# Attention: the two rows of a step added into one bank, half of each head's 16 output rows for each

## The chip, the cores and the metric

One NeuronCore of one Trainium2 chip runs the whole program in one launch. The metric is the device time in microseconds (us), the median of several executions. Its engines are TensorE (PE, with its weight loads as PEld), VectorE (DVE), ScalarE (ACT), GpSimd (POOL) and SyncE (SP), which here issues most of the transfers.

## What is computed

The program is a triangular-attention block followed by an MLP and a four-way Mamba block on x of shape (2, 64, 64, 256), float32. The change is in the attention:

```python
B, N, _, E = x_in.shape            # 2, 64, 64, 256
H = 8; d_k = E // H                # 32
q, k, v1, v2 = ((x_in @ W).reshape(B, N, N, H, d_k) for W in (Wq, Wk, Wv1, Wv2))
scores = jnp.einsum('bilhd,bljhd->biljh', q, k) / np.sqrt(d_k)
att = jax.nn.softmax(scores, axis=2)
out = jnp.einsum('biljh,bilhd,bljhd->bijhd', att, v1, v2)     # this line
attn_out = out.reshape(B, N, N, E) @ Wo
```

For each pair of heads, image b and row i, `out[i, j, d]` is a sum over l of `att[l, j] * v2[l, j, d] * v1[i, l, d]`: the elementwise product of the first two is formed for every d, and the sum over l, weighted with v1, is a matrix product.

## The kernel before

The attention works on one pair of heads at a time (4 pairs, `PAIRS`), and 128 partitions hold (head of the pair, l). For each pair there are two chunks c, one per image b, 8 in all (`NC`). A chunk has 64 rows i, taken two at a time: 32 steps a chunk, 256 steps t in all, one main loop on each engine.

In a step, DVE and POOL share the elementwise product (`product`, L306): DVE makes `av[t % 2][:, both rows, d 0..21, j]` from att and `v2ps` (in PSUM), POOL makes d 22 to 31 from `v2sb`. The two `av` buffers let them run one step ahead of PE: `need(dve, i_done, 2 * t - 2)` holds product t until the matmuls of step t - 2 are done. PE (`row`, L473 to L486) sums over l. The 32 values of d are cut into 4 strips of 8; for one row i, strip s is one fp32 matmul with 128x32 weights `w[:, i, s, :]` and 512 moving columns (8 d, 64 j), and its result goes to partitions 32 s to 32 s + 31 of a bank, so that the four strips of a row use four different quarters of the array's columns. The strips 0 and 1 need only DVE's part of `av`; strip 2 is the first that waits for POOL. Each fp32 matmul of this kind shows in the trace as two passes, each a weight load and a matmul.

The weights are v1 with one column per (head, d) and zeros for the other head: of the 32 columns of a strip, 8 are used for head 0 (0 to 7), 8 for head 1 (16 to 23); the others hold zeros. So a bank holds one row i, and half of its 128 partitions hold zeros; within a partition only the 64 columns of its own d are wanted. ACT copies each bank whole to `ev` (`evict`, L646 to L655), one copy a row. `ev` has two buffers of `EB` = 4 banks. When four rows are in a buffer, SP stores them (`store`, L258 to L265) with 8 DMAs of 8 partitions, 4 rows and 64 columns each. A store must have landed before its buffer is used again (`o_stored`).

There are 3 banks for the rows (`NB`). The weights are built by ACT from v1 (`build`), 8 rows at a time in two copies, one for each head.

In the same loop, for the next pair of heads, PE computes the scores (`scores`, L461: 16 groups of 8 matmuls of 64x64 tiles, in steps 0 to 10 of a pair, one and two groups in turn) and later the transposes of att (`turn`, L471, 16 groups of four); ACT copies the scores, takes the exponentials and copies the transposed att; DVE finds the minima and inverts the sums (L356, L365), POOL normalises (L327). This is so in the first three pairs (steps t 0 to 191); the last pair has only its own work. At the end of a chunk ACT copies the next chunk's v2 to `v2ps` in three pieces (`turn_v2`), each as soon as DVE has read the old one; DVE's first product of the new chunk is in three pieces too, each waiting for its copy.

SP's queue is in order: per chunk the loads of the chunk after (`load_v2`, two halves of `load_v1`) stand between the stores. Each engine runs its program in the order of the code; nothing else sets it. At the very end half of the last store is issued from ACT (`store_last`), and SP waits at L297 for every store to land; then the block ends on all engines and the MLP block begins.

## Time and profile before

| | |
|---|---|
| median of 3 runs | 2349.0 us (2346.99 to 2353.96) |
| the profiled execution | 2351.3 us, its span in the profile 2349.5 us |
| main loop of the attention, first to last matmul of L485 | 258.9 to 1092.7 us of the span |
| first matmul of the MLP block | 1099.8 us |
| DVE, PE, ACT, POOL busy over the span | 85%, 87%, 55%, 58% |

Times in the rows count from the start of the span. A busy PE in the table is a count of overlapping matmul records, not of work done. "x" is the number of instructions merged in a row. What ended an engine's idle time stands behind the arrow.

### The profile page before, as it was taken

What the parts mean: (1) busy time and instruction counts of PE and PEld (TensorE: products, weight loads), DVE (VectorE), ACT (ScalarE), POOL (GpSimd) and SP (SyncE); (2) the same over time, 40 slices, a digit from 0 to 9 for tenths busy, and PEclk for the clock granted to TensorE, in tenths of its full rate; (3) what the DMA queues carried; (4) which work ended last, traced back from release to release, by engine and by line L of the source; (5) the groups of instructions that cost most, each with busy time, mean ns of one, the idle gap of its engine ahead of it and who ended that gap; (6) DMA issues with size and microseconds to landing.
All of it is one profiled execution on the core that took longest, in us unless ns stands there. A gap on an engine that the chain in (4) does not pass through costs nothing. (4 is left out here: it accounts for less than half of the span.)

```text
span 2349.5 us, 43512 instructions
## 1 busy us (share of the span) xinstructions
PE 2033.5 (87%) x17008; PEld 1405.1 (60%) x17008; DVE 2001.5 (85%) x2292; ACT 1303.9 (55%) x2840; POOL 1358.6 (58%) x734
## 2 busy tenths in 40 slices
PE   8989977787788776665999997999999999999997
PEld 7868522232233221111787875888888888888886
DVE  4426799989999999996798885899989999999997
ACT  3337667767766785543232244656565665555553
POOL 1103699989998999996011001455555555666553
PEclk9999999999999999998999998999999999999997
DMA  6768512122321212301134222343222333433432
GB/s 233 249 216 237 145 33 55 42 56 46 66 54 29 38 20 38 94 17 27 54 101 137 81 64 59 68 88 81 74 73 73 90 82 97 108 91 93 105 93 64
DMA packets 300828, 203.98 MB, mean 87 GB/s; under 512 B 202064, under 2 KB 278864, under 8 KB 296528
## 3 DMA queue, kind: packets, MB, share of 16 engines
q1 hardware_dynamic: 282304, 146.51, 25.8%
q0 software_dynamic: 8704, 33.56, 3.9%
q10 hardware_dynamic: 9616, 21.14, 3.1%
q8 instruction: 135, 2.21, 0.4%
q14 instruction: 69, 0.57, 0.1%
HBM read 133.24 MB, written 67.90 MB: 86 GB/s over the span
## 5 line engine op out<-in xcount | busy, mean ns | idle before, releaser
L306 DVE TENSOR_TENSOR att_av<-att_att,att_v2ps 128x2816 f32<-128x2816 f32 (+2 forms) x288 | 775.6, 2753 | 29.4 <-PE att_bank L485 26.5
L306 POOL TENSOR_TENSOR att_av<-att_att,att_v2sb 128x1280 f32<-128x1280 f32 x256 | 744.3, 2933 | 45.6 <-PE att_bank L485 41.5
L485 PE MATMUL att_bank<-att_av,att_w 128*32 128x512 f32 x4096 | 551.0, 617 | 213.0 <-DVE att_av L306 189.8
L485 PEld LDWEIGHTS att_bank<-att_av,att_w 128*32 128x32 f32 x4096 | 138.6, 111 | 563.6 <-issue 282.7
L651 ACT ACTIVATE att_ev<-att_bank 128x512 f32<-128x512 f32 x512 | 296.8, 595 | 262.4 <-PE att_bank L485 218.3
L1864 DVE SCALAR_TENSOR_TENSOR mb_cv<-mb_bank,mb_cw,mb_cv 128x504 f32<-128x504 f32 (+2 forms) x480 | 351.5, 733 | 58.9 <-ACT mb_cv L1658 47.5
L1463 POOL TENSOR_TENSOR mb_y_lo<-mb_y,mb_y_hi 128x1024 fp32r<-128x1024 f32 x60 | 142.5, 2396 | 257.9 <-DVE mb_S L1873 257.9
L1534 PE MATMUL mb_bank<-dt_xT_hi,dt_win_hi 128*128 128x512 f32 x576 | 233.3, 405 | 27.5 <-DVE mb_cv L1864 24.4
L1534 PE MATMUL mb_bank<-dt_xT_lo,dt_win_hi 128*128 128x512 f32 x576 | 226.2, 393 | 0.0
L1534 PE MATMUL mb_bank<-dt_xT_hi,dt_win_lo 128*128 128x512 f32 x576 | 225.9, 392 | 0.0
L1658 ACT ACTIVATE mb_cv<-mb_bank,mb_cw 128x512 f32<-128x512 f32 x160 | 110.0, 690 | 194.6 <-PE mb_bank L1534 193.1
L1469 POOL TENSOR_TENSOR mb_S<-mb_S,mb_dskip 128x512 f32<-128x512 f32 x124 | 158.2, 1296 | 8.5 <-DVE mb_S L1880 8.5
L1873 DVE TENSOR_TENSOR_SCAN mb_S<-mb_dAb,mb_inj 128x512 f32<-128x512 f32 x128 | 149.7, 1211 | 3.2 <-DMA mb_dAb<-dA_rows 3.2
L1534 PEld LDWEIGHTS mb_bank<-dt_xT_hi,dt_win_hi 128*128 128x128 f32 x576 | 109.2, 190 | 62.1 <-DVE mb_cv L1864 38.5
L1446 POOL TENSOR_TENSOR mb_inj<-mb_diag,dt_dt 128x512 f32<-128x512 f32 x128 | 129.7, 1046 | 13.1 <-DVE mb_S L1873 13.0
L1676 ACT ACTIVATE mb_xc<-mb_cv,mb_cb 128x512 f32<-128x512 f32 x128 | 91.7, 716 | 69.3 <-DVE mb_cv L1864 69.3
L606 ACT ACTIVATE att_raw<-att_raw,att_least 128x64 f32<-128x64 f32 x384 | 128.5, 339 | 0.8
L1594 PE MATMUL mb_bank<-dt_wf_hi,mb_y_hi 128*128 128x256 f32 x512 | 128.8, 291 | 0.0
L1594 PE MATMUL mb_bank<-dt_wf_lo,mb_y_hi 128*128 128x256 f32 x512 | 126.0, 286 | 0.0
L1534 PEld LDWEIGHTS mb_bank<-dt_xT_hi,dt_win_lo 128*128 128x128 f32 x576 | 109.0, 189 | 24.1
L1004 PE MATMUL mlp_bank<-mlp_w,mlp_hid 128*128 128x256 f32 x512 | 118.4, 382 | 3.6 <-ACT mlp_hid L1081 3.6
L1534 PEld LDWEIGHTS mb_bank<-dt_xT_lo,dt_win_hi 128*128 128x128 f32 x576 | 109.2, 190 | 19.6
(199 smaller groups left out, 3864.4 us busy)
## 6 DMA issues: line engine op xcount, KB each, us to landing
att_xin<-in_x SPq DMA_DIRECT2D x32, 512.0 KB, 4.4
qk_t<-att_qk POOLq DMA_DIRECT2D x16, 1024.0 KB, 5.1
v<-att_vs POOLq DMA_DIRECT2D x16, 1024.0 KB, 5.6
mb_dAb<-dA_rows SPq DMA_DIRECT2D x32, 512.0 KB, 6.3
mb_dAb<-dA_cols SPq DMA_DIRECT2D x32, 512.0 KB, 5.7
mixed_t<-att_ev SPq DMA_DIRECT2D x1020, 8.0 KB
att_q<-qk_t ACTq DMA_DIRECT2D x32, 256.0 KB, 4.3
att_kb<-qk_t ACTq DMA_DIRECT2D x64, 128.0 KB, 2.9
```

What stands on the lines that cost most here:

```text
L306: return eng.tensor_tensor(av[t % 2][:, :, d0:d1, :], a.unsqueeze(2).broadcast_to((P, 2, d1 - d0, N)), v2.unsqueeze(1).broadcast_to((P, 2, ...
L485: mm = pe.matmul(bank[r % NB][s * M:(s + 1) * M, :], w[i // WB % 2][:, i % WB, s, :], av[r // 2 % 2][:, i % 2, s * STRIP_D:(s + 1) * STRIP ...
L606: ins = act.activation(a, a, ACT.Exp, scale=-1.0, bias=least[:, j, h:h + 1], accum_out=rsum[:, j, h:h + 1])
L651: act.activation(ev[e % 2][:, i % EB, :], bank[(c * N + i) % NB][:, :], ACT.Copy).then_inc(o_copied, 1)
L1004: mm = pe.matmul(OUT_[t // 2][:, (t % 2) * E:(t % 2 + 1) * E], hid[:, k, t * P:(t + 1) * P], w2[:, k, :], start=(i == 0), stop=(i == FT - 1))
L1446: pool.tensor_tensor(inj[:, p], diag[:, :].unsqueeze(1).broadcast_to((P, NH, L)), dtt[way(c)][:, c % NCHUNK * PAIR + p, :].unsqueeze(2).br ...
L1463: pool.tensor_tensor(y_["lo"][:, s, :], y[:, s, :], y_["hi"][:, s, :], ALU.subtract).then_inc(y_lo_ready, 1)
L1469: pool.tensor_tensor(S[:, p, :], S[:, p, :], dskip[way(c)][:, :, :].rearrange("p h t -> p (h t)"), ALU.add)\
L1534: mm = pe.matmul(PR_[b][:, :], win_[w][:, k, col:col + P], xT_[x][:, k, :], start=(n == 0), stop=(n == 3 * KT - 1))
L1594: pe.matmul(O_[t][:, 0:E], y_["hi"][:, m, t * P:(t + 1) * P], wf[way(c)][wn][:, m, :], start=(m == 0 and wn == "hi"), stop=False)
L1864: dve.scalar_tensor_tensor(out=dst, in0=src, scalar=cw[way(c)][:, m, TAPS - 1 - back:TAPS - back], in1=dst, op0=ALU.mult, op1=ALU.add)\
L1873: dve.tensor_tensor_scan(S[:, p, :], dAb[:, p, :], inj[:, p].rearrange("p h t -> p (h t)"), 0.0, ALU.mult, ALU.add).then_inc(scanned, 1)
```

## The change

Both rows of a step go into one bank. Of the 16 columns that a head has in a strip's 32 weights, row 0 of the step uses the first 8 and row 1 the last 8, the rest are zeros; the two matmuls of a strip, one per row, add up in the same 32 partitions (`start` on the first, `stop` on the second). The matmuls of a step now go strip by strip, both rows of a strip one behind the other. So:

- `row` becomes `rows`: still 8 matmuls a step with the same shapes, in another order, into one bank; `i_done` counts steps, and one `o_copied` covers a step.
- ACT has one eviction per step (256, not 512). A buffer of `ev` holds 4 steps, 8 rows.
- `build` writes the two rows of a step to different places, so it takes four copies of 128 elements in place of two of 256.
- A store covers 4 steps with 16 DMAs (8 d, 2 rows); 64 stores in place of 128. Its partitions per DMA, its size and the number of DMAs stay the same; in DRAM the four rows of one DMA are now every other row. The very last store is cut into two halves by steps: the first half is 16 DMAs of half the size once 2 of its 4 steps are evicted, the second half is 8 DMAs on SP and 8 on ACT.
- ACT copies all three pieces of the next v2 behind the single eviction of step 30, where the first piece stood between that step's two evictions.

```diff
-        w = [sb(f"w{u}", [P, WB, STRIPS, M]) for u in range(2)]
+        w = [sb(f"w{u}", [P, WB // 2, 2, STRIPS, M]) for u in range(2)]
...
             def store(c, e):
...
-                for d8 in range(STRIP_D // 2 if c * N + (e + 1) * EB == NC * N else STRIP_D):
-                    sp.dma_start(rows.rearrange("(x d) (i j) -> d x i j", d=STRIP_D, i=EB)[d8],
-                                 ev[e % 2][d8:P:16, :, d8 * N:(d8 + 1) * N]).then_inc(o_stored[e % 2], 16)
+                last = c * (N // 2) + (e + 1) * EB == NC * (N // 2)
+                for q0, q1 in ((0, EB // 2), (EB // 2, EB)) if last else ((0, EB),):
+                    sp.wait_ge(o_copied, c * (N // 2) + e * EB + q1)
+                    for d8 in range(STRIP_D // 2 if q1 - q0 < EB and q1 == EB else STRIP_D):
+                        for r in range(2):
+                            sp.dma_start(out_rows(c, e)[d8, r][:, q0:q1],
+                                         ev[e % 2][r * STRIP_D + d8:P:16, q0:q1, d8 * N:(d8 + 1) * N])\
+                                .then_inc(o_stored[e % 2], 16)
...
-            def row(c, i):
+            def rows(c, step):
...
                 for s in range(STRIPS):
-                    if i % 2 == 0 and s == 0:
-                        pe.wait_ge(av_by_dve, r // 2 + 1)
-                    if i % 2 == 0 and s == DD // STRIP_D:
-                        pe.wait_ge(av_by_pool, r // 2 + 1)
-                    mm = pe.matmul(bank[r % NB][s * M:(s + 1) * M, :], w[i // WB % 2][:, i % WB, s, :],
-                                   av[r // 2 % 2][:, i % 2, s * STRIP_D:(s + 1) * STRIP_D, :], start=True, stop=True)
+                    if s == 0:
+                        pe.wait_ge(av_by_dve, t + 1)
+                    if s == DD // STRIP_D:
+                        pe.wait_ge(av_by_pool, t + 1)
+                    for r in (0, 1):
+                        mm = pe.matmul(bank[t % NB][s * M:(s + 1) * M, :],
+                                       w[k % 2][:, i0 // 2, r, s, :],
+                                       av[t % 2][:, r, s * STRIP_D:(s + 1) * STRIP_D, :], start=(r == 0), stop=(r == 1))
...
-                evict(c, 2 * step)
-                if c + 1 < NC and step == N // 2 - 2:
-                    turn_v2(c + 1, 0)
-                evict(c, 2 * step + 1)
+                evict(c, step)
...
                 if c + 1 < NC and step == N // 2 - 2:
-                    turn_v2(c + 1, 1)
-                    turn_v2(c + 1, 2)
+                    for i in range(NP):
+                        turn_v2(c + 1, i)
```

PE, the second step of a pair before, and the scores behind it; a row of this listing is one or more fp32 matmuls (two passes each), the numbers behind names are buffers:

```order
L485 MATMUL att_bank2<-att_av1,att_w0 32x512 [waits att_av_by_dve]
L485 MATMUL att_bank2<-att_av1,att_w0 32x512
L485 MATMUL att_bank2<-att_av1,att_w0 32x512 [waits att_av_by_pool]
L485 MATMUL att_bank2<-att_av1,att_w0 32x512
L485 MATMUL att_bank0<-att_av1,att_w0 32x512 [waits att_o_copied]
L485 MATMUL att_bank0<-att_av1,att_w0 32x512 x3
L461 MATMUL att_x1<-att_kb0,att_q 64x128 [waits att_t_copied]
```

The same step now:

```order
L499 MATMUL att_bank1<-att_av1,att_w0 32x512 [waits att_av_by_dve]
L499 MATMUL att_bank1<-att_av1,att_w0 32x512 x3
L499 MATMUL att_bank1<-att_av1,att_w0 32x512 [waits att_av_by_pool]
L499 MATMUL att_bank1<-att_av1,att_w0 32x512 x3
L473 MATMUL att_x1<-att_kb0,att_q 64x128 [waits att_t_copied]
```

Strips 0, 1, 2, 3 of one row, then of the other, have become strip 0 of both rows, strip 1 of both rows, and so on: four passes of one quarter of the columns stand in a row, where there were two.

SP at the end of the attention, before (`store`), where L150 is the wait for all stores and the end of the block:

```order
L264 DMA mixed_t<-att_ev0 8x4x64 [waits att_o_copied]
L264 DMA mixed_t<-att_ev0 8x4x64 x7
L264 DMA mixed_t<-att_ev1 8x4x64 [waits att_o_copied]
L264 DMA mixed_t<-att_ev1 8x4x64 x3
L150 UNCONDITIONAL_BRANCH [waits att_head_loaded,att_o_stored1,att_o_stored0]
```

And now:

```order
L275 DMA mixed_t<-att_ev0 8x4x64 [waits att_o_copied]
L275 DMA mixed_t<-att_ev0 8x4x64 x15
L275 DMA mixed_t<-att_ev1 8x2x64 [waits att_o_copied]
L275 DMA mixed_t<-att_ev1 8x2x64 x15
L275 DMA mixed_t<-att_ev1 8x2x64 [waits att_o_copied]
L275 DMA mixed_t<-att_ev1 8x2x64 x7
L152 UNCONDITIONAL_BRANCH [waits att_head_loaded,att_o_stored1,att_o_stored0]
```

Behind the last full store there were 4 DMAs on SP, and there are 24 now; ACT has 8 where it had 4.

ACT at the end of a chunk, before (`evict`, `turn_v2`):

```order
L651 ACTIVATE att_ev1<-att_bank0 128x512 [waits att_i_done,att_o_stored1]
L633 ACTIVATE att_v2ps<-att_v2in 128x512 [waits att_v2_read]
L651 ACTIVATE att_ev1<-att_bank1 128x512 [waits att_i_done]
L633 ACTIVATE att_v2ps<-att_v2in 128x512 [waits att_v2_read]
L633 ACTIVATE att_v2ps<-att_v2in 128x384 [waits att_av_by_dve]
```

And now:

```order
L620 ACTIVATE att_raw,att_rsum<-att_raw,att_least 128x64 x2
L666 ACTIVATE att_ev1<-att_bank2 128x512 [waits att_i_done]
L620 ACTIVATE att_raw,att_rsum<-att_raw,att_least 128x64 x2
L666 ACTIVATE att_ev1<-att_bank0 128x512 [waits att_i_done]
L647 ACTIVATE att_v2ps<-att_v2in 128x512 [waits att_v2_read] x2
L647 ACTIVATE att_v2ps<-att_v2in 128x384 [waits att_av_by_dve]
```

The first piece of v2 stood behind the eviction of the step's first row; it stands behind the eviction of the whole step.

## Rows read from the trace of the kernel before

**Rows 1.** Groups of instructions, main loop: shapes, count, busy us, mean ns, idle us before

```profile
L306 DVE TENSOR_TENSOR att_av<-att_att,att_v2ps 128x2816 f32<-128x2816 f32 x240 | 725.3, 3078 | 26.6 <-PE att_bank L485 26.5
...
L651 ACT ACTIVATE att_ev<-att_bank 128x512 f32<-128x512 f32 x512 | 296.8, 595 | 262.4 <-PE att_bank L485 218.3 <-DMA mixed_t<-att_ev 42.3
```

**Rows 2.** What DVE waited for in the main loop: us in total, times, longest

```profile
DVE att_av L306 <- PE att_bank L485: 26.5, 30, 3.6
DVE att_rinv L365 <- ACT att_raw L606: 3.0, 3, 1.3
```

**Rows 3.** Timeline of one step: start us, us, engine, line, names, count, idle before

```profile
1069.59 0.19 PEld L485 LDWEIGHTS att_bank<-att_av,att_w 128*32 128x32 f32 x8 [1.95 <-issue]
1069.62 1.92 PE L485 MATMUL att_bank<-att_av,att_w 128*32 128x512 f32 x16 [1.07 <-DVE att_av L306]
1070.05 0.15 PEld L485 LDWEIGHTS att_bank<-att_av,att_w 128*32 128x32 f32 x4 [0.27 <-issue]
```

**Rows 4.** Timeline of PE: a step's matmuls, and the scores behind them

```profile
710.44 1.92 PE L485 MATMUL att_bank<-att_av,att_w 128*32 128x512 f32 x16
712.30 2.07 PE L461 MATMUL att_x<-att_kb,att_q 64*64 64x128 f32 x32
```

**Rows 5.** Timeline of PE in a step in which POOL is late, then transposes

```profile
851.78 1.05 PE L485 MATMUL att_bank<-att_av,att_w 128*32 128x512 f32 x4 [1.07 <-DVE att_av L306]
...
853.42 1.91 PE L485 MATMUL att_bank<-att_av,att_w 128*32 128x512 f32 x12 [0.59 <-POOL att_av L306]
...
855.27 0.66 PE L471 MATMUL att_x<-att_ident,att_raw 128*128 128x128 f32 x4
```

**Rows 6.** Stretches of 0.06 us in the Mamba block, L1581 alone: matmuls, weight loads in work

```profile
1764.88:1764.94 0.06, 0.06 (x10) 0.06 (x7) 1.00 0.00 0
1764.94:1765.00 0.06, 0.06 (x12) 0.06 (x11) 1.00 0.00 0
...
1765.06:1765.12 0.06, 0.06 (x16) 0.06 (x14) 1.00 0.00 0
```

**Rows 7.** What DVE waited for at 259-312, 469-513 and 683-735 us (steps with scores)

```profile
DVE att_av L306 <- PE att_bank L485: 5.4, 7, 1.1
...
DVE att_av L306 <- PE att_bank L485: 7.0, 5, 3.6
...
DVE att_av L306 <- PE att_bank L485: 3.5, 5, 0.9
```

**Rows 8.** Waits where ACT had waited for a store: PE at 480-500, DVE at 911-923 us

```profile
PE att_bank L485 <- ACT att_ev L651: 2.7, 1, 2.7
...
DVE att_av L306 <- PE att_bank L485: 2.5, 2, 2.2
```

**Rows 9.** Steps after a longer pause of PE; the first one's granted clock (PEclk)

```profile
304.43 4.80 PE L485 MATMUL att_bank<-att_av,att_w 128*32 128x512 f32 x28 [2.20 <-DVE att_av L306]
...
308.01 3.09 DVE L306 TENSOR_TENSOR att_av<-att_att,att_v2ps 128x2816 f32<-128x2816 f32 x1 [0.73 <-PE att_bank L485]
...
898.40 1.92 PE L485 MATMUL att_bank<-att_av,att_w 128*32 128x512 f32 x16 [1.84 <-DVE att_av L306]
...
303.50:309.00 5.50, 4.57 (x28) 0.69 0.04 7
```

**Rows 10.** Timeline where a pair ends: first piece of v2, and DVE's product behind it

```profile
467.29 1.06 ACT L633 ACTIVATE att_v2ps<-att_v2in 128x512 f32<-128x512 f32 x1
...
468.48 1.22 DVE L306 TENSOR_TENSOR att_av<-att_att,att_v2ps 128x1024 f32<-128x1024 f32 x1 [0.46 <-ACT att_v2ps L633]
```

**Rows 11.** The end of the attention: last stores, and SP's wait for them

```profile
1093.33 2.40 SPq L264 DMA_DIRECT2D mixed_t<-att_ev  x4
1093.34 3.40 ACTq L704 DMA_DIRECT2D mixed_t<-att_ev  x4
...
SPq L297 <- DMA mixed_t<-att_ev: 2.1, 1, 2.1
```

**Rows 12.** SP's issues of another pattern of three dimensions, four in a row

```profile
1848.95 2.88 SPq L1363 DMA_DIRECT2D mb_xin<-x  x4
```

More of the change, by code:

```diff
@@ L222, in block_attention @@
         NC = PAIRS * B
+        NE, STORED = N // 2 // EB, 16 * 2 * STRIP_D
         GROUPS_PER_STEP = [1, 2] * 5 + [1] + [0] * 53
@@ L550, in _ @@
                         pe.wait_ge(v_by[e], 2 * XN)
-                for i in (0, 1):
-                    row(t // (N // 2), t % (N // 2) * 2 + i)
+                rows(t // (N // 2), t % (N // 2))
                 if n < PAIRS:
@@ L700, in store_last @@
             def store_last():
[L701 to L702 removed]
+                act.wait_ge(o_copied, NC * (N // 2))
                 for d8 in range(STRIP_D // 2, STRIP_D):
[L704 removed]
+                    for r in range(2):
+                        act.dma_start(out_rows(NC - 1, NE - 1)[d8, r][:, EB // 2:],
+                                      ev[1][r * STRIP_D + d8:P:16, EB // 2:, d8 * N:(d8 + 1) * N]).then_inc(o_stored[1], 16)
             xT_hi(0)
```

66 lines of the change are left out of this document (34 added, 32 removed).

## The prediction

> **What bounds the kernel now.** I read the page's share table and the groups of the main loop first, then what DVE waited for, then single steps as timelines. The whole change lies in the attention's main loop (258.9 to 1092.7 us) and its end. In the loop DVE is the bound: 240 whole products take 725.3 us, 3.02 us a step [rows 1], and DVE waits only 26.5 us for PE and 3.0 us for ACT's exponentials [rows 2]. So all that ACT, PE and SP could save here is about 30 us, and ACT's halved evictions are worth nothing by themselves: 256 x 0.6 = 152 us go [rows 1], on an engine that waits anyway.
>
> A usual step is in [rows 3]: DVE's product ends, PE's matmuls start at 1069.62 and are over 1.92 us later. The 16 passes are not one after the other. The weight loads come eight at once at 1069.59, then four at 1070.05: the four strips, each on its own quarter of the columns, run together, and a round (one pass of every strip) takes 0.43 us. Four rounds are 1.72 us, and 0.2 us pass until the result is there. DVE's product t + 2 waits for that, but only 3.02 us after the end of product t, so PE has 3.02 - 0.15 - 1.92 = about 0.95 us to spare. In the 33 steps with scores (11 in each of three pairs) it has none: matmuls start at 710.44, scores at 712.30, with nothing between [rows 4]. These steps take 3.4 us, and DVE waits 5.4, 7.0 and 3.5 us there [rows 7]. Here PE is the bound.
>
> **The change, part by part.**
>
> PE's order. The eight matmuls are the same, but strip 0 now has four passes in a row before strip 1 has its first. Each strip still has four rounds of work; the question is whether all strips start together. They do only if PE can look past the passes that stand before. That it does look past some is seen already: in the order of the program strip 3's first pass stands seventh, behind three that cannot start yet, and it starts with the first [rows 3]. How far it looks is seen in the Mamba block. There (L1581) 16 matmuls on one pair of 64x64 tiles are followed by 16 on the other pair, which is free. If PE saw them all, four tiles would work all the time. They don't: up to 1764.94 seven weight loads are in work, then 11, and 14 at the end of the first 16, at 1765.12 [rows 6]. A round there is 64 / 512 x 0.43 = 0.054 us, so the second pair comes in three rounds before the end, with 2 x 3 = 6 passes of the first not yet started. So PE looks about 7 or 8 waiting passes ahead. Numbering a step's passes 1 to 4 for strip 0, 5 to 8 for strip 1, 9 to 12 and 13 to 16: when pass 1 starts, pass 5 is the fourth waiting, pass 9 the seventh (2, 3, 4, 6, 7, 8 before it), pass 13 the tenth. Pass 13 is too far. One round later 2, 6 and 10 have gone, 13 is the seventh, and starts. Five rounds, not four: a step's matmuls take 1.92 + 0.43 = 2.35 us.
>
> The Trainium skill speaks to this in two ways that do not agree (TensorE: Matmul & The Clock Gate). Its part on the engine's queue gives it 64 entries as a partial reorder window; a step is 32 instructions, so by that all strips start together and the round is not lost (rival A). Its part on packing small matmuls, under what overlaps, says matmuls start and end strictly in program order; by that the strips come out one after the other (rival C). The trace bears neither out in full: the first would have four tiles at work throughout in [rows 6], the second would not let strip 3 start with strip 0 in [rows 3].
>
> What the round costs. Where DVE bounds, 0.95 us to spare become 0.5: nothing. A step with a transpose behind it: 0.15 + 4 + 1 rounds (2.15) and 0.6 to 0.66 us [rows 5] is 2.9, under 3.02: nothing. Where POOL is late, strips 0 and 1 do both rows before it comes, and after it the rest takes four rounds, 1.91 us as now [rows 5]: nothing. Where PE bounds: 33 steps, and one more block at each of the three ends, 36 x 0.43 = **+15.4 us**.
>
> Evictions. One of 0.6 us after the whole step, in place of one after each row. Banks and `ev` last twice as long in steps. A store had to land within some 8.2 us (two steps, and the third up to its first row); it takes 8 x 0.6 + 2.1 = 6.9 us [rows 11], and the loads between the stores break that. Now it has five steps, 15 us, for 16 x 0.6 + 2.1 = 11.7 us: 3.4 us to spare instead of 1.3, and the lag is made up twice as fast. I take it that ACT's late stores no longer reach PE or DVE. They cost 2.7 us (PE) and 0.5 us behind it, and 2.5 us (DVE) [rows 8]: **-5.9 us**.
>
> The exponentials have 0.6 us more a step, but begin 0.5 us later: of DVE's 3.0 us [rows 2] I take **-2 us** (0 to -3).
>
> The clock. After pauses of 2.2 us PE ran at 0.69 of full speed over the next 5.5 us, its level of 1.2 GHz for most of it, after a pause of 1.84 us it did not fall [rows 9]. Five rounds shorten a pause of 2.2 to 1.77 us, so I expect fewer of these steps; the first of them costs DVE 0.73 us [rows 9], and I count four, 2.3 us together. If they stay they cost one more round of 0.85 us, +3.4. I take **-2 us**.
>
> The four `build` copies: 128 elements instead of 256, four instead of two, at most +0.4 us in four steps, hidden by the 0.6 us a step that ACT gains.
>
> The end of a chunk. The first piece of v2 started at 467.29, behind a row's eviction; it now starts behind the step's, about 0.65 us later, and DVE, which waited 0.46 us for it already, waits for it [rows 10]. Part of it is given back at the second piece. At the three ends of a pair 0.45 us, at the last chunk 0.4, elsewhere a reduction of DVE covers it: **+1.8 us**.
>
> The end. Nothing is behind SP's last stores that could hide them: the block ends with SP's wait. Now 4 DMAs on SP (2.4 us) and 4 on ACT (3.4 us) follow the last eviction, then 2.1 us [rows 11], together 4.5 us from 1093.33. After the change, with T the last eviction: the last full store is ready at T - 12, and its 16 DMAs of 0.61 us run to T - 2.2; 16 of the first half run to T + 7.5, 8 more to T + 12.4; with 2.1 us of waiting T + 14.5. T is itself 0.4 us later. 14.5 + 0.4 - 4.5 = **+10.3 us**. Half-size DMAs aren't in the trace. The nearest rows are the stores themselves (0.6 us, 8x4x64) and another pattern of three dimensions with more in it (0.72 us each, [rows 12]), so the size matters little and I keep 0.61. Were they issued in 0.4 us it would be +5.3 us; at 0.72 us +12.9.
>
> Sum: 15.4 - 5.9 - 2 - 2 + 1.8 + 10.3 = +17.6 us on the profiled 2351.3 us, 2368.9. The median of the runs is 2.3 us lower, so **2366.6 us**, 0.75% slower.
>
> **The rivals.**
>
> A. All four strips start together (PE looks ten or more passes ahead). Then the 15.4 us go: 2351.2 us, no change within 0.3%. Against it is [rows 6]; for it, that another tile shape may be looked through differently.
>
> B. Faster. As A, and ACT's early evictions also take away all DVE waiting outside the steps with scores: 26.5 + 3.0 - (5.4 + 7.0 + 3.5) = 13.6 us, with the 4.1 us of the stores' price in the second scores stretch, 17.7 us in all instead of the 9.9 us I count: 2343.4; with the cheap end (5.3) 2338.4 us. It decides from the rounds: at five it is lost. Against it: half of these waits are for POOL, not ACT, as in [rows 5].
>
> C. PE looks less far. If strip 2 is a round late too and strip 3 two, six rounds: +15.4 again, and the steps with transposes then pass DVE's 3.02 us, by 0.3 to 0.4 us in some 40 steps: about 2395 us. If the strips follow one another wholly, ten rounds: 4.3 us a step everywhere, 1.3 x 223 + 2.6 x 33 = +375 us, about 2730 us.
>
> D. SP becomes the bound: the stores' DRAM side now has a stride. At 0.61 us it needs 9.8 us of 12.1; it would bind from 0.75 us. At 0.72 us [rows 12] it would not, but the 3.4 us to spare would be gone and the 5.9 us not won, and the end costs 12.9: 2375 us.
>
> **How the numbers follow.** The forecast (2357 to 2376 for its own terms) has 0.62, A 0.15, B 0.04, C 0.09, D 0.10. Predicted is 2366 us. The range, 2347 to 2379, takes in A and D and leaves out B and C. A measurement here can tell 0.3%, 7 us, from no change: faster is below 2342 (B's cheap half, 0.03), same up to 2356 (A, the rest of B, and a forecast whose end is cheap, 0.19), slower 0.78.
>
> **What would show it.** Right: a step in the last chunk whose matmuls take 2.35 us, weight loads first for three strips and then for the fourth; steps with scores at 3.8 us in place of 3.4; no wait of ACT for a store that reaches DVE; SP's stores running some 12 us past the last eviction. Wrong: 1.92 us for a step (A), or 2.8 and more (C); stores whose issue takes 0.7 us (D); an end as short as before.

## The result, and the profile after

The changed kernel takes 2361.9 us (median of five, 2361.4 to 2363.1) where the kernel before takes 2350.4 us: a ratio of 1.0051, with an interval of 1.0039 to 1.0063. It is 11.5 us slower. 2366 us were predicted (2347 to 2379, and 0.78 for slower). The side and the range hold; of the sum behind them one large term is wrong and another was some four times too small, and the two errors partly cancel.

The table cuts the profiled executions at three places that can be read in any timeline: the first matmul into `bank`, the end of the last eviction, and the first matmul of the MLP that follows the attention. Times in us; the median and the ratio are those of the runs. Each ratio is taken to runs of the kernel before that belong to the same set; the sets ran on different chips, so two rows are compared better by their ratios.

| kernel | main loop | end | behind it | median | ratio to before |
|---|---|---|---|---|---|
| before | 834.4 | 6.5 | 1249.7 | 2350.4 | |
| before, once more | 826.4 | 6.5 | 1255.9 | 2350.0 | 0.9994 |
| after | 830.3 | 16.5 | 1254.7 | 2361.9 | 1.0051 |
| strips innermost | 830.2 | 16.5 | 1254.8 | 2361.2 | 1.0037 |
| last stores shared | 828.5 | 11.5 | 1255.8 | 2358.4 | 1.0029 |
| v2 first | 819.4 | 16.5 | 1254.6 | 2351.1 | 1.0004 |
| v2 first, last stores shared | 820.0 | 11.5 | 1252.3 | 2347.3 | 0.9985 |
| v2 first, last two steps stored one by one | 822.0 | 13.4 | 1250.1 | 2347.1 | 0.9983 |
| v2 first, last store whole | 817.9 | 9.5 | 1251.1 | 2344.1 | 0.9962 |
| before with v2 first | 833.3 | 6.5 | 1254.2 | 2350.3 | 0.9993 |
| before with a longer end | 827.7 | 14.3 | 1256.4 | 2357.5 | 1.0029 |

Two things stand in it before any reading of rows. The end is 10.0 us longer, nearly the whole difference. And the loop of the kernel before is not one number: in four executions (two of the kernel as it is, one with a longer end, one with a copy moved) it took 826 to 834 us. A term of a few microseconds is therefore read from the waits, not from a difference of two loops. What follows the attention varies by up to 7 us between executions of the same code, and says nothing on the change.

The groups of the main loop after the change (line, engine, names, shapes, count | busy us, mean ns | idle us before them and who ended it), and what DVE waited for there:

```profile
L318 DVE TENSOR_TENSOR att_av<-att_att,att_v2ps 128x2816 f32<-128x2816 f32 x240 | 725.3, 3077 | 23.5 <-PE att_bank L499 23.3
...
L666 ACT ACTIVATE att_ev<-att_bank 128x512 f32<-128x512 f32 x256 | 152.7, 597 | 382.9 <-PE att_bank L499 376.7 <-DMA mixed_t<-att_ev 5.8
...
DVE att_av L318 <- PE att_bank L499: 23.3, 30, 1.2
DVE att_av L318 <- ACT att_v2ps L647: 4.7, 4, 1.3
```

And DVE's wait for v2 in the kernel before:

```profile
DVE att_av L306 <- ACT att_v2ps L633: 2.3, 7, 0.5
```

DVE's product costs what it did [rows 1]. The evictions are half as many, 152.7 us in place of 296.8, and ACT waits for stores 5.8 us in place of 42.3. DVE no longer waits for the exponentials at all (3.0 us in [rows 2]), but 4.7 us for v2, where it waited 2.3.

One step after the change, to be held against [rows 3]:

```profile
1087.55 0.21 PEld L499 LDWEIGHTS att_bank<-att_av,att_w 128*32 128x32 f32 x8 [2.06 <-ACT att_ev L666]
1087.58 1.95 PE L499 MATMUL att_bank<-att_av,att_w 128*32 128x512 f32 x16 [1.18 <-DVE att_av L318]
1088.01 0.18 PEld L499 LDWEIGHTS att_bank<-att_av,att_w 128*32 128x32 f32 x4 [0.25 <-issue]
1088.43 0.18 PEld L499 LDWEIGHTS att_bank<-att_av,att_w 128*32 128x32 f32 x4 [0.25 <-issue]
```

Eight weight loads at once, then four and four, and 16 passes in 1.95 us: all four strips start together. There is no fifth round.

The end, and SP's wait behind it, against [rows 11] (here the last eviction was over at 1090.20):

```profile
1078.10 25.52 SPq L275 DMA_DIRECT2D mixed_t<-att_ev  x40
...
1090.22 6.17 ACTq L720 DMA_DIRECT2D mixed_t<-att_ev  x8
...
SPq L309 <- DMA mixed_t<-att_ev: 1.1, 1, 1.1
```

SP issues 40 transfers in a row, the last of them 13.4 us past the last eviction; 1.1 us later they have landed.

### The profile page after: what moved, and what is told of

Its sections match the earlier page's. It is cut to its first block and busy times, and to the rows that moved or that the text cites. A ratio compares the mean times of both kernels' runs of the same rounds, so it can differ in the third digit from the quotient of the medians.

```text
span 2361.3 us, 43335 instructions
## 1 busy us (share of the span) xinstructions
PE 2041.7 (86%) x17008; PEld 1427.5 (60%) x17008; DVE 2001.0 (85%) x2292; ACT 1178.1 (50%) x2712; POOL 1358.7 (58%) x734
## 5 line engine op out<-in xcount | busy, mean ns | idle before, releaser
L499 PEld LDWEIGHTS att_bank<-att_av,att_w 128*32 128x32 f32 x4096 | 157.3, 110 | 540.7 <-issue 304.2
L666 ACT ACTIVATE att_ev<-att_bank 128x512 f32<-128x512 f32 x256 | 152.7, 597 | 382.9 <-PE att_bank L499 376.7
L1548 PE MATMUL mb_bank<-dt_xT_hi,dt_win_hi 128*128 128x512 f32 x576 | 233.8, 406 | 27.0 <-DVE mb_cv L1878 23.9
```

The lines of the kernel that those rows point to most:

```text
L499: mm = pe.matmul(bank[t % NB][s * M:(s + 1) * M, :], w[k % 2][:, i0 // 2, r, s, :], av[t % 2][:, r, s * STRIP_D:(s + 1) * STRIP_D, :], sta ...
L666: act.activation(ev[e % 2][:, step % EB, :], bank[t % NB][:, :], ACT.Copy).then_inc(o_copied, 1)
L1548: mm = pe.matmul(PR_[b][:, :], win_[w][:, k, col:col + P], xT_[x][:, k, :], start=(n == 0), stop=(n == 3 * KT - 1))
```

## How far TensorE looks

The fifth round was the prediction's largest term (+15.4 us), so three kernels were made to find the rule that it had wrong, and one to see whether the order of the strips costs anything.

**Strips innermost.** The changed kernel with row 0 of all strips first, then row 1, as the passes stood before:

```diff
-                for s in range(STRIPS):
-                    ...
-                    for r in (0, 1):
+                for r in (0, 1):
+                    for s in range(STRIPS):
```

> The changed kernel with the step's matmuls in the old order: the four strips of row 0, then the four of row 1, into the one bank. Theory W (PE looks past more than 20 instructions, so the order of the strips costs nothing): the step keeps its 1.92 us and four rounds, the time is the changed kernel's, 2361 to 2363 us or ratio 1.005. The step of the prediction (strip 3 a round late when strips stand one behind the other) would make this kernel faster than the changed one by 15 us; the changed kernel's trace speaks against it already.

2361.2 us, ratio 1.0037 (1.0023 to 1.0050), beside 1.0051 (1.0039 to 1.0063) with the strips outermost; loop and end are the same to 0.1 us. With four passes a strip the order of the strips costs nothing that these runs can show.

**Eight passes a strip.**

```diff
-                    for r in (0, 1):
+                    for r in (0, 1, 0, 1):
```

> Extra work: each strip's pair of matmuls is done twice over (start again at the third), so that a strip's last pass stands 12 passes and more behind its first one, and strip 3's first pass is the 25th of a step instead of the 13th; the output is the same. It asks how far TensorE looks. If its reach is counted in a dozen or so passes waiting, strip 3 starts only when passes of strips 0 to 2 have gone, the eight weight loads at a step's start are six or fewer and a step takes more than eight rounds (9 to 10, 3.9 to 4.3 us). If it reaches over 24 passes and as many loads, all four strips start within 0.1 us, and a step's 32 passes take eight rounds, 3.5 us. The time of the whole is near 2560 us if TensorE (3.5 us of rows and 1.7 of scores or transposes a step, 128 steps... some 30 of them bound by it already at 3.4) sets the stretches with other work in them; it is not what the run is for.

It took 3538 us (one execution, as of the next two kernels), and neither guess was near. The weight loads of one step near the loop's start (columns: start us, us, engine, line, names, shapes, count, idle before):

```profile
271.12 0.14 PEld L499 LDWEIGHTS att_bank<-att_av,att_w 128*32 128x32 f32 x2
271.57 0.11 PEld L499 LDWEIGHTS att_bank<-att_av,att_w 128*32 128x32 f32 x1 [0.32 <-issue]
272.00 0.11 PEld L499 LDWEIGHTS att_bank<-att_av,att_w 128*32 128x32 f32 x1 [0.32 <-issue]
272.43 0.11 PEld L499 LDWEIGHTS att_bank<-att_av,att_w 128*32 128x32 f32 x1 [0.32 <-issue]
272.86 0.14 PEld L499 LDWEIGHTS att_bank<-att_av,att_w 128*32 128x32 f32 x3 [0.32 <-issue]
273.29 0.14 PEld L499 LDWEIGHTS att_bank<-att_av,att_w 128*32 128x32 f32 x2 [0.29 <-issue]
273.72 0.14 PEld L499 LDWEIGHTS att_bank<-att_av,att_w 128*32 128x32 f32 x2 [0.29 <-issue]
274.18 0.11 PEld L499 LDWEIGHTS att_bank<-att_av,att_w 128*32 128x32 f32 x1 [0.32 <-issue]
```

Two loads (the running pass of strip 0 and the next one), then one a round: for four rounds strip 0 works by itself. In the fifth, at 272.86, there are three: one for strip 0 and two for strip 1, which starts. From there on 3, 2, 2, 1 come again and again, at most two strips at work at a time, and a step by itself takes 20 rounds for 32 passes. A window that counts the waiting passes of all strips together cannot do this: strip 1 stands behind seven waiting passes here and waits, and in the changed kernel strip 3 stands behind nine and starts at once.

A rule that gives both: passes are handed out in the order of the program, each to its own strip; a strip holds four of them, the running one among them; and a pass whose strip is full holds up everything behind it. With four passes a strip nothing is ever held up. With eight, the fifth to eighth wait until one of the first has gone, and strip 1 gets its first pass when the eighth of strip 0 is handed out, as strip 0's fifth starts: four rounds late.

The same rule reads [rows 6] in another way. There the second pair of tiles came in three rounds before the end of the first, with six passes not yet started. The prediction took the six for one queue of seven or eight. By the rule they are three waiting on each of two tiles, beside the running one: four on each.

**Six passes a strip**, for which the rule and the window say different things, in numbers:

```diff
-                    for r in (0, 1):
-                        mm = pe.matmul(..., start=(r == 0), stop=(r == 1))
+                    for k2, r in ((0, 0), (1, 0), (2, 1)):
+                        mm = pe.matmul(..., start=(r == 0), stop=(k2 != 1))
```

> The changed kernel, each strip with three matmuls (row 0's twice, the second one starting again, then row 1's), so six passes a strip in a row, and 24 a step. Theory F (each strip has a queue of four passes, the running one among them; passes are handed out in program order, and a pass whose strip is full holds up all behind it): strip 1 starts two rounds behind strip 0, strip 2 two behind it, strip 3 six rounds behind strip 0; a step by itself takes twelve rounds of 0.43 us, 5.2 us, and its weight loads come in rounds of 2, 1, 3, 2, 4, 2, 4, 2, 2, 1, 1. With eight passes a strip that rule gives 2, 1, 1, 1, 3, 2, 2, 1, 3, 2, 2, 1, 3, 2, 2, 1, 1, 1, 1, as the run with eight showed. Theory W (a window over the waiting passes of all strips together): one that lets strip 3 start at once with four passes a strip reaches nine passes or more, and with six a strip strips 0 and 1 then start together and strip 2 by the first or second round; 8 or 9 rounds, 3.9 us at most. By F the whole takes some 2750 us, by W some 2500.

```profile
1160.79 0.14 PEld L499 LDWEIGHTS att_bank<-att_av,att_w 128*32 128x32 f32 x2 [0.17 <-issue]
1161.25 0.11 PEld L499 LDWEIGHTS att_bank<-att_av,att_w 128*32 128x32 f32 x1 [0.32 <-issue]
1161.68 0.14 PEld L499 LDWEIGHTS att_bank<-att_av,att_w 128*32 128x32 f32 x3 [0.32 <-issue]
1162.11 0.14 PEld L499 LDWEIGHTS att_bank<-att_av,att_w 128*32 128x32 f32 x2 [0.29 <-issue]
1162.53 0.17 PEld L499 LDWEIGHTS att_bank<-att_av,att_w 128*32 128x32 f32 x4 [0.29 <-issue]
1162.99 0.14 PEld L499 LDWEIGHTS att_bank<-att_av,att_w 128*32 128x32 f32 x2 [0.29 <-issue]
1163.42 0.17 PEld L499 LDWEIGHTS att_bank<-att_av,att_w 128*32 128x32 f32 x4 [0.29 <-issue]
1163.88 0.14 PEld L499 LDWEIGHTS att_bank<-att_av,att_w 128*32 128x32 f32 x2 [0.29 <-issue]
1164.31 0.14 PEld L499 LDWEIGHTS att_bank<-att_av,att_w 128*32 128x32 f32 x2 [0.29 <-issue]
1164.77 0.11 PEld L499 LDWEIGHTS att_bank<-att_av,att_w 128*32 128x32 f32 x1 [0.32 <-issue]
1165.20 0.11 PEld L499 LDWEIGHTS att_bank<-att_av,att_w 128*32 128x32 f32 x1 [0.32 <-issue]
```

The counts are the ones written down: 2, 1, 3, 2, 4, 2, 4, 2, 2, 1, 1. The whole took 2799 us (2750 expected by this rule, 2500 by the window).

**Eight passes a strip, strips innermost**, the same work as with eight passes a strip above, in another order (the edit against the kernel with the strips innermost):

```diff
-                for r in (0, 1):
+                for k2 in range(4):
+                    r = k2 % 2
                     for s in range(STRIPS):
```

> The same double work as in the run with each strip's pair done twice (32 passes a step), but with the strips innermost: row 0 of all strips, row 1 of all strips, and both once more. Theory F (a queue of four passes for each strip): no strip is ever more than four passes behind when the next strip's pass is handed out, all four work all the time, eight rounds, 3.5 us a step by itself and near 3.5 us a step in the last chunk; the whole some 2520 us, against 3538 with the strips outermost. If the double accumulation itself (a second start in the same bank) is what made that run slow, this one is as slow, 3500 us.

```profile
1085.25 0.19 PEld L500 LDWEIGHTS att_bank<-att_av,att_w 128*32 128x32 f32 x8 [0.67 <-issue]
1085.71 0.16 PEld L500 LDWEIGHTS att_bank<-att_av,att_w 128*32 128x32 f32 x4 [0.27 <-issue]
```

Eight at once, then four a round, as in the kernel after, and the next step's eight follow 3.50 us behind, at 1088.75; 2542.6 us against 3538, near the 2520 expected. The doubled work was not what made the other slow, its order was. These are the second set of numbers that the rule gave ahead and that came out.

What the rule counts in is open: every matmul here is two passes, so four passes and two matmuls are the same in all these runs. The Trainium skill (TensorE: Matmul & The Clock Gate, Part 3, the mechanism and what overlaps) has a 64-deep window that pulls weight loads ahead, and matmuls that start and end strictly in program order. The traces agree with neither as a whole: matmuls of a free strip overtake waiting ones of another (1.95 us for 16 passes), but only as long as no strip before them is full, and with eight passes a strip the first weight load of strip 1, the 17th instruction of the step, came four rounds late.

## The end

Two kernels change only what is stored when.

**The kernel before with a longer end.** Sixteen transfers of 8 KB more on SP ahead of its last store. Their bytes are not part of the result.

```diff
+                    if c == NC - 1 and e == N // EB - 1:
+                        for k in range(16):
+                            sp.dma_start(v_dram[8 * k:8 * k + 8, 0:EB * N].rearrange(...),
+                                         ev[0][k % 8:P:16, :, 0:N]).then_inc(o_stored[0], 16)
...
```

SP's wait at the end counts them too.

> The kernel before, with 16 more DMAs of the stores' size (8 KB, to a part of the v scratch that is read no more) issued on SP ahead of the last store; nothing else is changed. SP then ends 16 x 0.61 = 9.8 us later, less the 1.2 us it had idle: the way from the last eviction to the MLP's first matmul becomes 6.5 + 8.6 - 1.0 (ACT's own stores ended last before) = 14.1 us, +7.6 us. Theory N: the time is +7.6 us, ratio 1.0032. Theory D: the later start of the next blocks costs another 5 us, +12 to +13 us, ratio 1.0055.

The end grew from 6.5 to 14.3 us, by 7.8, and the whole by some 7 us (2357.5 us, ratio 1.0029 with 1.0018 to 1.0039). Nothing hides the end, and nothing behind it multiplies it: the interval is 4 to 9 us, and a cost of 12 to 13, the other guess, is outside.

**The last stores shared** between SP and ACT: of the store before the last ACT issues eight of the 16 transfers, of the first half of the last store four.

```diff
+                if c == NC - 1 and step in (28, 29):
+                    store_part(NE - 2, 0, EB, 8 + 4 * (step - 28), 12 + 4 * (step - 28))
+                if c == NC - 1 and step == 30:
+                    store_part(NE - 1, 0, EB // 2, 12, 16)
...
```

> The changed kernel with the stores of its last two buffers shared out: SP issues 8 of the 16 DMAs of the last but one, 12 of the first half of the last, 8 of the second half; ACT issues the others, four behind each of the evictions of steps 28, 29 and 30, and 8 at the end. Worked out from 0.61 us an issue on SP: SP is done 6.2 us after the last eviction instead of 12.4, so the end is 6 us shorter than the changed kernel's 16.5 us from last eviction to the MLP's first matmul: 10 to 10.5. Theory N: the median follows, 2356 us, ratio 1.0025. Theory D: it falls by more, as the blocks behind the attention return to 1249.7 us: 2351 us, ratio 1.000.

2358.4 us, ratio 1.0029 (1.0018 to 1.0041); the end fell from 16.5 to 11.5 us, where 10 to 10.5 were expected, and the median by 3.5 us (2.8 beside the strips innermost, whose loop and end are those of the changed kernel). Sharing helps less than the count of transfers promises, since an issue becomes dearer while the other engine issues too. SP in this kernel beside ACT, then SP alone at the end of the changed one:

```profile
1088.91 5.17 SPq L278 DMA_DIRECT2D mixed_t<-att_ev  x7
...
1097.56 6.06 SPq L275 DMA_DIRECT2D mixed_t<-att_ev  x10
```

Seven in 5.17 us are 0.74 us each, ten in 6.06 us are 0.61. The first few issues of such a stretch still take 0.61; the 0.76 us that an expectation below uses comes from a row of SP with a wait of 1.7 us inside. The Trainium skill (Perfetto Trace Analysis, "DMA Instruction — HWDGE") says that the block that makes the descriptors is shared and has a wait for its lock. The dearer issues agree with that; a wait for a lock by itself is not in these rows.

## The pair ends

That the loop is no shorter although ACT's late stores are gone needed a loss of equal size. The places were three, where a pair of heads ends: the copy of v2's first piece to PSUM and what follows it (ACT's row, DVE's two, PE's step; then a stretch with its length, busy us and instructions of PE, PEld, DVE, ACT and POOL, PE's granted clock, DMA share and GB/s):

```profile
468.50 2.90 ACT L647 ACTIVATE att_v2ps<-att_v2in 128x512 f32<-128x512 f32 x3
...
469.73 6.21 DVE L318 TENSOR_TENSOR att_av<-att_att,att_v2ps 128x1024 f32<-128x1024 f32 x4 [1.29 <-ACT att_v2ps L647]
476.73 3.09 DVE L318 TENSOR_TENSOR att_av<-att_att,att_v2ps 128x2816 f32<-128x2816 f32 x1 [0.79 <-PE att_bank L499]
...
473.09 3.54 PE L499 MATMUL att_bank<-att_av,att_w 128*32 128x512 f32 x16 [2.39 <-DVE att_av L318]
...
472.00:475.00 3.00, 1.91 (x12) 0.73 (x16) 3.00 (x3) 0.00 (x0) 2.49 (x1) 0.66 0.81 131
```

The copies start at 468.50, behind the eviction of step 30. Counted from the moment at which DVE was ready for the first one, that is 0.8 us later than in [rows 10]: DVE now waits 1.29 us for it instead of 0.46. PE's pause ahead of the next rows is 2.39 us instead of the 1.84 us of [rows 9]; behind it the clock is granted at 0.66 in that stretch, a mix that is the 1.2 GHz level from some point on, and the 16 passes take 3.54 us instead of 1.95. DVE waits 0.79 us for them at 476.73. The stretch with scores that follows is bound by PE, so a step that PE lost there isn't made up: the next of DVE's 0.76 us waits for the bank comes already at 483.57, where the kernel before (second execution) came to its first at 488.42, and there are five of them, not four.

The kernel with the last stores shared has the same code here, and at its first pair end the clock did not fall:

```profile
471.19 1.95 PE L502 MATMUL att_bank<-att_av,att_w 128*32 128x512 f32 x16 [2.38 <-DVE att_av L321]
...
472.00:475.00 3.00, 3.00 (x36) 1.53 (x32) 3.00 (x2) 1.69 (x6) 2.34 (x2) 1.00 0.12 23
```

DVE waits 1.27 us for v2 there too, but not for the slow step, and then four times 0.76 us, not five. So of what such an end costs, 1.3 us is the late copy and 1.55 us the clock. Of the twelve ends of a pair or of the chunk at 991 us in the three executions without the move below, the clock fell at eleven.

**v2 first.** The changed kernel, the first copy ahead of the eviction of step 30:

```diff
+                if c + 1 < NC and step == N // 2 - 2:
+                    turn_v2(c + 1, 0)
                 evict(c, step)
                 ...
-                    for i in range(NP):
+                    for i in range(1, NP):
```

> The changed kernel, with one thing put back: at a pair's end the first of the three copies of v2 to PSUM stands on ScalarE ahead of the eviction of step 30, not behind it, as it stood before between the two evictions of that step. Theory P (the pair ends cost the loop its 3.4 us): in the changed kernel VectorE waits 1.3 us for that copy three times (469.7, 681.4, 893.0), TensorE's pause ahead of the next rows grows from 1.84 to 2.4 us, its clock falls to the 1.2 GHz level for one step, and the lead over TensorE that VectorE had until some 12 us into the following stretch is gone. With the copy first VectorE's wait for v2 falls from 4.7 to under 2.5 us in sum, the pause is under 2 us again, its wait for the bank falls from 23.3 to about 18 us, the loop takes 824 to 827 us instead of 830.3, and the median is 2356 to 2358. Theory Q (the 3.4 us come from what every step has new: weights with columns apart, sixteen passes in one bank, evictions in halved number): the wait for v2 falls, the wait for the bank rises by as much, the loop stays at 829 to 831 us and the median at 2361.

```profile
465.73 1.11 ACT L647 ACTIVATE att_v2ps<-att_v2in 128x512 f32<-128x512 f32 x1 [0.89 <-DVE att_av L318]
...
458.48 15.38 DVE L318 TENSOR_TENSOR att_av<-att_att,att_v2ps 128x2816 f32<-128x2816 f32 x9 [1.19 <-PE att_bank L499]
...
471.02 1.95 PE L499 MATMUL att_bank<-att_av,att_w 128*32 128x512 f32 x16 [1.06 <-DVE att_av L318]
...
DVE att_av L318 <- PE att_bank L499: 18.0, 24, 1.2
```

The copy starts at 465.73; DVE's next nine instructions go over the pair's end without a wait (the new chunk's first product is three of them), PE's step starts after 1.06 us and takes 1.95 us at full clock. DVE's waits fall from 28.0 to 18.0 us and the one for v2 is gone, also the 2.3 us that the kernel before had. The loop is 10.9 us shorter, the median 2351.1 us (1.0004, with 0.9996 to 1.0013). The expectation had the mechanism and half the size: 2356 to 2358 us. It stopped at the first wait behind the pause. Between this kernel and the changed one each of the first two pair ends costs 1.29 us (v2) + 0.79 us (slow step) + 0.76 us (one wait more behind it) = 2.8 us; the third, with no scores behind it, costs 1.29 + 0.79 = 2.1 us, and one more chunk's end 0.84 us for v2. That is 8.6 us of the 10.0 us by which DVE's waits differ; the rest is in steps behind other pauses, where the clock fell here less often. At none of these ends did it fall in any of the four changed kernels with v2 first (this one and the next three).

**Both edits**, v2 first and the last stores shared:

> Two edits at once: the first v2 copy ahead of the eviction of step 30, and SyncE's and ScalarE's halves of the last two stores (the edit that by itself gave 2358.4). If the two losses are separate places, the gains add: 3 us of the end and what the first edit gives, so under theory P 2352 to 2355 us, under theory Q 2358. From last eviction to the first matmul of the MLP some 11.5 us.

2347.3 us (0.9985, with 0.9976 to 0.9993), loop 820.0, end 11.5. The losses are in separate places and add up; it is faster than the kernel before, by less than 0.3%.

**The last two steps stored one by one**, both rows in a transfer of 16 partitions:

```diff
+                if last:
+                    store_step(sp, EB - 2, 0, STRIP_D)
+                    store_step(sp, EB - 1, 0, STRIP_D // 2)
...
```

> The kernel with both edits, and the last two steps stored one by one, each by eight transfers that carry both of its rows (16 partitions of one step) instead of sixteen that carry one row of both steps: behind the last eviction SyncE and ScalarE then issue four transfers each, as before the change, not eight. If the end is the sum of what the two queues still have to issue, the stretch from last eviction to the MLP's first matmul falls from 11.5 to between 6.5 and 8.5 us, and the median comes out at 2347 to 2351 (theory P) or 2353 to 2355 (theory Q). If a transfer of 16 partitions costs its issuer as much as two of 8, it stays at 11.

```profile
1069.52 15.31 SPq L284 DMA_DIRECT2D mixed_t<-att_ev  x20
1084.87 7.42 SPq L229 DMA_DIRECT2D mixed_t<-att_ev  x12
```

A miss: the end took 13.4 us, not 6.5 to 8.5. A transfer of 16 partitions is not dearer (7.42 / 12 = 0.62 us), but SP came late to it. Its twenty older transfers were not out before 1084.8, 2.9 us past the last eviction at 1081.94. It was not the transfers of the last step that made the end, but the backlog: 48 transfers in the last eight steps, 32 of them on SP, where it had 28 in the run before.

**The last store whole**, with v2 first: no halves, one store of four steps, eight transfers on each engine.

```diff
-                for q0, q1 in ((0, EB // 2), (EB // 2, EB)) if last else ((0, EB),):
+                for q0, q1 in ((0, EB),):
                     ...
-                    for d8 in range(STRIP_D // 2 if q1 - q0 < EB and q1 == EB else STRIP_D):
+                    for d8 in range(STRIP_D // 2 if last else STRIP_D):
```

> The changed kernel with the first v2 copy ahead of the eviction of step 30, and with the last store whole: not two halves of two steps (sixteen transfers each) but one store of four steps after the last eviction, eight of its transfers on SyncE and eight on ScalarE. In the kernel with stores by step SyncE still had a backlog (its stores ran 10.4 us past the last eviction, at 0.76 us each while ScalarE issued too, and 0.62 us alone), though only eight transfers belonged to the last step. Theory (the end costs what is still to be issued, and 48 transfers in the last eight steps are too many): with 32, nothing is left over, eight on each queue at 0.6 to 0.76 us are 5 to 6.1 us, and 2.1 us of landing follow; from last eviction to the MLP's first matmul 9 to 10 us in place of 16.5, the median 2351.1 - 7 = 2344 us. Rival (it is the data of the last step that counts, and a whole store moves more bytes after it): 12 us or more, 2347 us.

```profile
1077.16 5.29 SPq L275 DMA_DIRECT2D mixed_t<-att_ev  x8
...
1077.16 6.40 ACTq L720 DMA_DIRECT2D mixed_t<-att_ev  x8
```

32 transfers in the last eight steps instead of 48; the end takes 9.5 us (9 to 10 expected) and the median is 2344.1 us (2344 expected), a ratio of 0.9962 with 0.9950 to 0.9974. This kernel is faster than both, by 7.6 us the kernel before, and by some 18 us (medians) to 21 us (ratios) the changed one. It is not the last word on the end: the kernel before, with eight transfers behind the last eviction in place of 16, has one of 6.5 us.

**The kernel before with v2 first**, to see whose gain it is:

```diff
-                evict(c, 2 * step)
                 if c + 1 < NC and step == N // 2 - 2:
                     turn_v2(c + 1, 0)
+                evict(c, 2 * step)
```

> The kernel before, with its first v2 copy moved ahead of the first of the two evictions of step 30. It asks whether the 10 us that this move gave the changed kernel are to be had without the change. In the kernel before VectorE waits for v2 2.3 us in seven places, and the clock does not fall behind the pause there (1.84 us). If what the move repairs is the changed kernel's own loss, it brings here 2.3 us at most, 2348 to 2350 us; the loop is 825 us, 5 us longer than the changed kernel's with the same move (819.4), and that difference is what the change itself gains. If the move is worth 10 us here too, 2340 us, the change itself gains nothing in the loop.

2350.3 us, ratio 0.9993 (0.9982 to 1.0004): 1.4 us by the medians, with an interval from a gain of 4 us to a loss of 1. The 2.3 us of waits for v2 are gone; a gain of 10 us is excluded. So what the move repairs is, in the main, the changed kernel's own loss. Its loop was expected at 825 us and took 833.3 in the profiled execution; the waits say why. Of it, and of the second run of the kernel before:

```profile
DVE att_av L306 <- PE att_bank L485: 27.0, 26, 4.7
DVE att_rinv L365 <- ACT att_raw L606: 4.1, 3, 1.7
...
ACT att_ev L651 <- DMA mixed_t<-att_ev: 42.9, 14, 6.4
...
DVE att_av L306 <- PE att_bank L485: 17.2, 22, 1.2
...
ACT att_ev L651 <- DMA mixed_t<-att_ev: 36.8, 14, 5.7
```

ACT waits for stores some 40 us in both, but in one of them a wait of 4.7 us reaches DVE, as one of 3.6 us did in [rows 7], and in the other none over 1.2 us does. The late store and the slow step behind it make some 3 to 5.5 of the 7 to 8 us by which loops of the kernel before differ; the rest are waits of 0.2 to 0.8 us, most of them behind a fall of the clock. In the seven profiled executions with one eviction a step ACT waited 1.4 to 8.0 us for stores, no wait for the bank over 1.2 us reached DVE, and their loops agree within 2 us (three without the move) and 4 us (four with it).

**The kernel before, once more**, is the measure of how far a single execution can be trusted:

> The kernel before once more, on the chip and in the call of the next three. The two traces so far add up like this: attention loop 4.1 us shorter, end of the attention 10.0 us longer, and 5 to 6 us more in the MLP and Mamba blocks, whose code did not change. If those are scatter of a single execution (theory N), this profile's blocks behind the attention lie between the two seen so far (1249.7 us before, 1254.6 us after, from the MLP's first matmul to the end), and its ratio is 1.000. If they are a lasting effect of what happens at the end of the attention (theory D), this profile repeats 1249.7 within 1 us.

2350.0 us, 0.9994 (0.9985 to 1.0003), with the loop 8.0 us shorter than in the first profile and what follows 6.2 us longer.

## Why the prediction was right, and where it was wrong

The side and the size of the whole came out because the end, +10.3 us, was right and stands almost alone in the result, and for the rest by luck: without the fifth round the same sum gives 2351.2 us, no change, and what brings the measured time back to 2361.9 are the pair ends, which it had too small. The steps, one by one, with the predicted term first:

- **A fifth round, +15.4: measured 0.** The step that failed is the reading of [rows 6]: six passes not yet started were taken for one queue over all tiles and carried over to four strips, where nine have to wait. They were three on each of two tiles. The mechanism of rival A was the true one, at 2351 us, and it had 0.15. Its time was missed mainly because A shared the mis-sized term of the pair ends.
- **ACT's late stores, -5.9, and the exponentials, -2: measured about -7 together.** Worked out from medians: v2 first is 1.0 us slower than the kernel before with an end 10 us longer, so its loop gains 9 us; of these some 2 are the v2 waits that the kernel before had. DVE's wait for the exponentials, 3.0 to 4.4 us in four executions of kernels with two evictions a step, is 0 in all with one. ACT's wait for stores went from 42.3 to 5.8 us, but what that gives depends on the execution: a late store reached DVE in two of those four and in the other two not, so in those the term was worth nothing.
- **The clock, -2: not borne out.** The term held that the clock falls after a pause of 2.2 us and holds after 1.84, and that a fifth round would shorten the pause. There is no fifth round, and the pauses in question are 2.17 to 2.20 us, where they were 2.20. At one place the two kernels show the same pause and a different clock. Of the kernel before (second run), then of the one after:

```profile
305.85 1.92 PE L485 MATMUL att_bank<-att_av,att_w 128*32 128x512 f32 x16 [2.20 <-DVE att_av L306]
...
306.00:309.00 3.00, 1.93 (x20) 0.50 (x17) 3.00 (x2) 1.74 (x5) 2.43 (x2) 1.00 0.04 8
...
305.84 5.28 PE L499 MATMUL att_bank<-att_av,att_w 128*32 128x512 f32 x32 [2.18 <-DVE att_av L318]
...
306.00:309.00 3.00, 3.00 (x16) 0.69 (x13) 2.69 (x1) 0.00 (x0) 1.29 (x1) 0.50 0.07 14
```

  2.20 us and full clock; 2.18 us and 0.50, the lower level, for two steps. The first execution of the kernel before had 2.20 us at this place and 0.69 [rows 9]. So the length of the pause alone does not decide it, nor does the kernel. Behind its first steps the loop has stretches of some 3.5 us at the lower level, which the granted clock shows: 10, 6, 4 and 6 in the four executions of kernels with two evictions a step, and 8, 10 and 8 in the three of the changed one and its like, of which 4, 4 and 3 are at the ends of pairs and chunks. Away from those ends they are 4, 6 and 5: no sign that the change brings more of them, nor, from so few executions, fewer. Why the clock falls in one execution and not in another was not tried.
- **The chunk ends, +1.8: measured +6 to +8.5 against the kernel before.** The medians give 8.5 (10.8 us between the changed kernel and v2 first, less the 2.3 us of waits that the kernel before has), the waits at these ends 6.3 (8.6 less 2.3). Right place, right waiting engine, and DVE's wait for v2 itself was nearly right: it grew by 2.4 us, from 2.3 to 4.7. But the term ended at that wait. PE's pause grew with it from 1.84 to 2.39 us, the clock fell behind it, and the stretch behind is bound by PE: another 3.9 us of waits for the bank.
- **The end, +10.3: measured +10.0.** 40 transfers in 25.5 us are 0.64 us each, where 0.61 was taken. The details shifted: the issues that SP made beside ACT's took up to 0.74 us, and 1.1 us of landing followed instead of 2.1.
- **The price of `build`, nothing: so it was.** The group of the copies (L659) in the profile has 253 of 299 ns, 63.7 us, on an engine that waits 376.7 us for PE.

The sum with the measured terms is 0 - 7 + 8.5 + 10.0 = 11.5 us. That it meets the 11.5 of the medians proves nothing: the two terms of the loop are differences of medians through the same third kernel, each good to some 2 us, and what is wrong in one is made good in the other. The waits are the independent check. DVE's are 23.9 us in the second execution of the kernel before, 28.0 in the changed kernel and 18.0 with v2 first, and the loops are 826.4, 830.3 and 819.4 us. The first of these differences, 4.1 us, is +6.3 at the ends of pairs and chunks, -4.4 for the exponentials, and +2.2 for the bank elsewhere.

Of the rivals, B (faster) counted the end too, but gave the loop 17.7 us for early evictions where the medians show about 7. C (six or ten rounds) cannot be with four passes a strip; it is what eight passes a strip do. D (SP's issue dearer) is true only while ACT issues too, 0.74 us in place of 0.61, which in this kernel is behind the last eviction.

## What to carry to other kernels

A queue read from one place of a trace has to be read per resource before it is carried to another: here four passes for each tile, not eight for the engine. So fp32 matmuls packed like these can stand strip by strip as long as a strip has no more than four passes in a row, and above that the strips belong in the innermost loop. When an eviction, a copy or a store is moved, follow the delay until somebody has slack again: a copy 0.8 us late cost nearly three times that, 2.2 us, through a pause of TensorE, its clock and a stretch that it bounds. And at the end of a phase count the transfers still to be issued over the last few steps, not only those of the last one: splitting the last store in halves made more issues than it hid.

## What the runs showed of the hardware that was not expected

- Each strip of columns holds four passes (or two matmuls of two passes each), the running one among them, and a full strip holds up the passes of all others behind it: 1.95 us for 16 passes with four in a row a strip, and for 32 passes 20 rounds of 0.43 us with eight in a row against eight rounds with the strips innermost (3538 and 2543 us for the whole kernel).
- Two engines that issue transfers at once slow each other: 0.74 us an issue, but for the first few, against 0.61 alone. A transfer of 16 partitions of one step costs no more than one of eight partitions of two or four steps (0.62 us).
- The same pause of PE is followed by the full clock in one execution and by the 1.2 GHz level in another, at 2.2 us and also at 2.4 us.
